# Hidden units in order in two expert stages, and routing choices made once behind the chunk loop

## The chip, the cores and the metric

The kernel runs on one core of a Trainium2 chip, as one program. The metric is the device time of one execution in microseconds, median of several runs. Everything is float32 unless a form says bf16.

## What is computed

Two layers, each a graph attention over 6250 nodes (256 features, 206250 edges) followed by a mixture of 8 experts, with residual additions. The change touches the expert halves only. Layer 0 takes the best two experts of a token, layer 1 the best one with a capacity per expert:

```python
logits = xt @ Wr + br                       # xt: 6250 x 256, Wr: 256 x 8
probs = softmax(logits); top_p, top_idx = top_k(probs, 2)
weights = top_p / top_p.sum(-1)
h = gelu((xn * ln_g + ln_b) @ W1[e] + b1[e])    # 256 -> 1024
y = h @ W2[e] + b2[e]                           # 1024 -> 256
out = sum of weights * y over the chosen experts
# layer 1: argmax of the softmax, relu in place of gelu, no scale and shift,
# tokens past the capacity of their expert are handled by position
```

## The kernel before, in words

The program is a sequence of phases: a plan of the edges, then per layer a node phase, an edge phase and `ffn_phases` (line 1272), which has two stages, routing and experts. Between stages all engines meet at a barrier.

**Routing** (lines 1292 to 1690). The 6250 tokens are 49 tiles of 128 (`NT`), in 7 chunks (`R`) of 7 tiles. SyncE loads the rows `xs` and the attention sums `ag` of a chunk (three `ag` buffers), stores the new rows (`keep_rows`, line 1358) and the scaled rows `xn` with their weights to `xb` (`keep_normed`, line 1362); its queue is one ordered list, so each store's wait holds the loads that stand behind it. GpSimd (POOL) adds the bias to each chunk (line 1420). VectorE runs `combine` (line 1519: sums divided, added to the rows, mean and variance) and `factors` (line 1547: scale and offset from ScalarE's root), and for the chunk before also `scores` (line 1560: logits, their maximum, the difference) and `choices` (line 1571: softmax, the chosen experts one-hot in `oh`, weights into `xn`, and `pick`). These work on 7 x 8 = 56 columns. In a chunk ScalarE takes the root (line 1469), the exponent of the chunk before (line 1473), scales 7 tiles (line 1482) and copies 7 transposed tiles out of PSUM (line 1488). Root and exponent need different tables, so each chunk has two table loads. TensorE transposes (line 1432) and makes the logits (line 1438).

Behind the loop TensorE counts the picks (lines 1451 and 1452), VectorE turns the counts into a slot for each choice (lines 1619 to 1648), and 7 chunks of one-hot matrices give the map from slots to tokens: `low` (line 1655), `low` times the token's lane as `lowp` (line 1657) and, per choice, `high` (line 1661), all on VectorE, two buffers each, multiplied on TensorE (lines 1460, 1461). Then come the block table and the map's decoding (lines 1663 to 1690).

**Experts** (lines 1692 to 1920). Tokens of one expert form blocks of 256 (`TB`). All engines loop over pairs of blocks, with two buffers of everything. SyncE loads a block's expert: `w1`, `w2`, `b1`, `b2` (lines 1742 to 1745), two blocks ahead, released by `s_yc` when VectorE has read a block's result. GpSimd gathers the tokens (line 1763), and scatters the result (line 1788 adds in DRAM in layer 0, line 1791 writes in layer 1). TensorE does per block 8 times 2 matmuls of the first product (line 1820), 4 transposes of the next block (line 1805) and 16 matmuls of the second (line 1831); the trace holds two records for each f32 matmul, so a block shows x32, x4 and x32. ScalarE applies the function with `b1` as bias (line 1843), VectorE scales the next block's transposes into `xT` (lines 1851, 1854), multiplies weights (`take`), adds `b2` (line 1896) and scales by the weight. In layer 1 it also replaces non-finite values (line 1914).

Hidden unit number p * 8 + j is unit p of group j. So each partition's part of `w2` and `b1` is one run in DRAM, and the stationary operand of line 1820 is every eighth column of `w1`:

```python
w1[:, k, c, :].rearrange("p (m j) -> p j m", j=FC)[:, j, :]       # line 1821
one(names["w2"]).rearrange("a (p j) d -> (a p) j d", j=FC)        # line 1743
one(names["b1"]).rearrange("a (p j) -> (a p) j", j=FC)            # line 1744
```

What sets the order: each engine's list is written out by hand, and semaphores are counted per block (`hold`, line 67). `done` (line 1495) makes VectorE wait for its own instruction.

Of the kernel before, what the change touches and what calls it, by code (L numbers as in the profile page):

```python
# [6 lines left out]
F32 = mybir.dt.float32  # L7
# [3 lines left out]
ALU = mybir.AluOpType  # L11
ACT = mybir.ActivationFunctionType
# [1259 lines left out]
def ffn_phases(nc, io, dr, layer, src, rows_in, out):  # L1272
# [13 lines left out]
    with ExitStack() as outer:  # L1286
# [5 lines left out]
        with ExitStack() as ctx:  # L1292
# [54 lines left out]
            s_w, s_const, s_zero, s_bias, s_agu, s_chain, s_stat, s_var, s_std, s_fac, s_xn = (  # L1347
                sem(n) for n in ("w", "const", "zero", "bias", "agu", "chain", "stat", "var", "std", "fac", "xn"))
            s_t, s_xT, s_l, s_soft, s_exp, s_wg, s_pick, s_cnt, s_low, s_lowp, s_map, s_done, s_kept = (
                sem(n) for n in ("t", "xT", "l", "soft", "exp", "wg", "pick", "cnt", "low", "lowp", "map", "done", "kept"))  # L1350
            block = ctx.enter_context(nc.Block())

            @block.sync
            def _(sp):
                tiles = lambda c: slice(c * R, (c + 1) * R)
                lines = lambda c: slice(c * R * P, (c + 1) * R * P)

                def keep_rows(c):
                    sp.wait_ge(s_agu, c + 1)
                    sp.dma_start(rows_in[lines(c), :].rearrange("(t p) d -> p t d", p=P), xs[:, tiles(c), :]).then_inc(s_kept, 16)  # L1360

                def keep_normed(c):
                    sp.wait_ge(s_wg, c + 1)
                    sp.wait_ge(s_xn, R * (c + 1))
                    sp.dma_start(xb[lines(c), :].rearrange("(t p) d -> p t d", p=P), xn[:, tiles(c), :]).then_inc(s_kept, 16)

                rest = N - (NT - 1) * P
                for c in range(R):
                    if first and c == R - 1:
                        sp.wait_ge(s_zero, 2)  # L1370
                        sp.dma_start(xs[:, c * R:NT - 1, :], src[c * R * P:(NT - 1) * P, :].rearrange("(t p) d -> p t d", p=P)).then_inc(s_x[c], 16)
                        sp.dma_start(xs[0:rest, NT - 1, :], src[(NT - 1) * P:N, :]).then_inc(s_x[c], 16)
                    else:
                        sp.dma_start(xs[:, tiles(c), :], src[lines(c), :].rearrange("(t p) d -> p t d", p=P)).then_inc(s_x[c], 16)
                    if c == 0:
                        sp.dma_start(bias[:, :], io["L0_gnn_bias" if first else "L1_gnn_bias"].partition_broadcast(P)).then_inc(s_w, 16)
                    if c >= AG:
                        keep_rows(c - AG)
                    sp.dma_start(ag[:, c % AG, :, :], dr["agg"][lines(c), :].rearrange("(t p) d -> p t d", p=P)).then_inc(s_ag[c % AG], 16)
                    if c == 0:  # L1380
                        sp.dma_start(wr[:, :, :], io[names["wr"]].rearrange("(c p) e -> p c e", p=P)).then_inc(s_w, 16)
                        sp.dma_start(br[:, :], io[names["br"]].partition_broadcast(P)).then_inc(s_w, 16)
                    if c > AG:
                        keep_normed(c - AG - 1)
                for c in range(R - AG, R):
                    keep_rows(c)
                    keep_normed(c - 1)
                sp.wait_ge(s_zero, 2)
                sp.dma_start(rows_in[NP:NP + TB, :].rearrange("(p s) d -> p (s d)", p=P), zero[:, :]).then_inc(s_kept, 16)
                keep_normed(R - 1)  # L1390
                sp.wait_ge(s_kept, 16 * (2 * R + 1))
# [31 lines left out]
            def _(pe):  # L1423
# [24 lines left out]

                pe.wait_ge(s_pick, R)
                picks = pick[:, :, :].rearrange("p t e -> p (t e)")  # L1450
# [14 lines left out]
            def _(act):  # L1465
# [4 lines left out]

                def powers(c):
                    act.wait_ge(s_soft, c + 1)
                    nc.scalar.activation(pr[:, c * R:(c + 1) * R, :], tmp[:, c * R:(c + 1) * R, :], ACT.Exp).then_inc(s_exp, 1)

                for c in range(R):
                    roots(c)
                    if c:
                        powers(c - 1)
                    act.wait_ge(s_fac, c + 1)
# [3 lines left out]
                    for k in range(R):  # L1483
# [4 lines left out]
                        nc.scalar.copy(xT[:, t % XP, :, :], ps_x[:, t % XP, 0:D].rearrange("p (c n) -> p c n", c=DC)).then_inc(s_xT, 1)  # L1488
                powers(R - 1)

            @block.vector
            def _(v):
# [63 lines left out]

                wide = lambda col: col.unsqueeze(2).to_broadcast([P, R, EXP])
                each = lambda row: row.unsqueeze(1).to_broadcast([P, R, EXP])

                def scores(c):  # L1560
                    cs = slice(c * R, (c + 1) * R)
                    v.wait_ge(s_l, R * (c + 1))
                    if first:
# [6 lines left out]

                def choices(c):
                    cs = slice(c * R, (c + 1) * R)
                    v.wait_ge(s_exp, c + 1)
                    p, q = pr[:, cs, :], tmp[:, cs, :]
# [33 lines left out]
                for c in range(R):  # L1608
                    combine(c)
                    if c:  # L1610
                        scores(c - 1)
                    factors(c)
                    if c:
                        choices(c - 1)
                scores(R - 1)
                choices(R - 1)
                v.wait_ge(s_cnt, 1)
# [32 lines left out]
                for c in range(R):  # L1650
                    k = c % 2
                    if c >= 2:
                        v.wait_ge(s_map, c - 1)
                    lows = slot[:, 2, c * R:(c + 1) * R, :].rearrange("p t n -> p (t n)")
                    done(nc.vector.tensor_tensor(low[:, k, :, :], iotal[:, :].unsqueeze(1).to_broadcast([P, R * top, P]),
                                                 lows.unsqueeze(2).to_broadcast([P, R * top, P]), ALU.is_equal))
                    nc.vector.tensor_scalar(lowp[:, k, :, :], low[:, k, :, :], iotan[:, 0:1], None, ALU.mult).then_inc(s_lowp, 1)
                    for j in range(R * top):
# [33 lines left out]
        with ExitStack() as ctx:  # L1692
# [5 lines left out]
            w1 = sb("w1", [P, 2, DC, FF], F32)  # L1698
            w2 = sb("w2", [P, 2, FC, D], F32)
            b1 = sb("b1", [P, 2, FC], F32)  # L1700
            b2 = sb("b2", [P, 2, D], F32)
# [21 lines left out]
            s_sc = [sem(f"sc{k}") for k in range(2)]  # L1723
            s_gx = [sem(f"gx{k}") for k in range(2)]
            s_gi, s_si, s_cur, s_add, s_mul, s_fl, s_pq, s_free = (sem(n) for n in ("gi", "si", "cur", "add", "mul", "fl", "pq", "free"))
            n_sc = 16 * SUB
            n_ldx = 16 * SUB
            n_ldw = 16 * 4
            n_ldg = 16 * 2
# [5 lines left out]
            def _(sp):  # L1735
                def load(b, k):
# [5 lines left out]
                    sp.dma_start(w1[:, k, :, :], one(names["w1"]).rearrange("a (p c) f -> (a p) c f", c=DC)).then_inc(s_ldw[k], 16)  # L1742
                    sp.dma_start(w2[:, k, :, :], one(names["w2"]).rearrange("a (p j) d -> (a p) j d", j=FC)).then_inc(s_ldw[k], 16)  # L1743
                    sp.dma_start(b1[:, k, :], one(names["b1"]).rearrange("a (p j) -> (a p) j", j=FC)).then_inc(s_ldw[k], 16)  # L1744
                    sp.dma_start(b2[:, k, :], one(names["b2"]).rearrange("a d -> (a d)").partition_broadcast(P)).then_inc(s_ldw[k], 16)

                for k in range(2):
                    load(k, k)
# [50 lines left out]
            def _(pe):  # L1799
                pe.wait_ge(s_const, 2)  # L1800

                def turn(k):
# [4 lines left out]
                    mm.then_inc(s_t, 1)  # L1807

                pe.wait_ge(s_ldx[0], n_ldx)
                turn(0)  # L1810
                pairs = pe.value_load(cnt_i[0:1, 0:1], min_val=1, max_val=(nblk_max + 1) // 2)
                with pe.Fori(0, pairs) as i:
                    for k in range(2):
                        hold(pe, s_ldw[k], i * n_ldw + n_ldw, s_pp)
                        hold(pe, s_xT, i * 2 + (k + 1), s_pp)
                        for j in range(FC):

                            hold(pe, s_act, i * (2 * FC) + (k * FC + j + 1), s_pp)
                            for c in range(DC):
                                mm = nc.tensor.matmul(ps_h[:, j % 4, 0:TB],  # L1820
                                                      w1[:, k, c, :].rearrange("p (m j) -> p j m", j=FC)[:, j, :],
                                                      xT[:, k, c, :], start=(c == 0), stop=(c == DC - 1))
# [24 lines left out]
            def _(v):  # L1847
# [9 lines left out]
                def take(b, k):  # L1857
# [5 lines left out]
                    nc.vector.tensor_tensor(wt[:, k, :], wt2[:, k, 0, :], wt2[:, k, 1, :], ALU.add)  # L1863

                def sources(b, k):
                    nc.vector.tensor_copy(gidx[:, k, :], who[:, bass.ds(b, 1), 0, :]).then_inc(s_gi, 1)
# [6 lines left out]
                for n, value in enumerate((0.0, 10000.0, -10000.0)):  # L1873
                    nc.vector.memset(bound[:, n, :], value).then_inc(s_fl, 1)
                v.wait_ge(s_fl, 3)
                v.sem_inc(s_yc, 1)
                v.wait_ge(s_t, 1)
                if first:
# [6 lines left out]
                with v.Fori(0, pairs) as i:  # L1885
                    for k in range(2):
                        hold(v, s_t, i * 2 + (k + 2), s_pv)
                        if first:
                            hold(v, s_ldg[1 - k], (i + k) * n_ldg + n_ldg, s_pv)
                        affine(1 - k)  # L1890
                        take(i * 2 + (k + 1), 1 - k)
# [74 lines left out]
```

## Time and profile before

| | |
|---|---|
| median of 3 runs | 6250.21 us (6245.75 to 6252.14) |
| the profiled execution | 6253.11 us |
| its span, first to last instruction | 6251.4 us |
| granted TensorE clock, mean | 0.883 |
| TensorE busy | 4504.6 us, 72% of the span |
| VectorE busy | 3544.0 us, 57% |
| ScalarE busy | 1454.2 us, 23% |
| GpSimd busy | 3674.1 us, 59% |

PE is TensorE's matmuls, PEld its weight loads, DVE VectorE, ACT ScalarE, POOL GpSimd, SP SyncE. The shares are means over stages with different limits: layer 0's routing lies from 2377 to 2584 us, its experts to about 3425, layer 1's routing from 5624 to 5795 and its experts to the end. Tile names in rows have the stage's prefix (`r_`, `x_`), out<-in. A timeline row merges neighbours of one line (xN).

### The profile page before, as it was taken

The numbers are of one execution on the slowest core, as the hardware profiler recorded it, in microseconds if no ns is written. First come the engines' busy times: TensorE is split into PE (matmuls) and PEld (weight loads), VectorE is DVE, ScalarE is ACT, GpSimd is POOL, SyncE is SP. The second block draws the span as 40 slices with busy tenths as digits, with TensorE's granted clock in tenths as the row PEclk, the third lists the DMA queues.
The fourth block names the chain that finished last, engine by engine and source line by source line (L and its number), as shares of the span: only waits on it lengthen the run. The fifth ranks groups of instructions, "written<-read, shape, count | busy, mean of one in ns | idle before, by whom it ended". The sixth has DMA issues, their size and how long they took to land. (4 is left out here: it accounts for less than half of the span.)

```text
span 6251.4 us, 96537 instructions
## 1 busy us (share of the span) xinstructions
PE 4504.6 (72%) x19217; PEld 3440.8 (55%) x19217; DVE 3544.0 (57%) x6578; ACT 1454.2 (23%) x3118; POOL 3674.1 (59%) x3755
## 2 busy tenths in 40 slices
PE   0678888888888885699998446565565655664898
PEld 0345555555555554599998334354453444554898
DVE  6678888888888877521221335344454443547444
ACT  1333333333333323122222201011110110113222
POOL 1577777777777751133333277777777777741333
PEclk9899999999999995799999668788787887885999
DMA  7566666666666644366666555555555555535555
GB/s 227 183 164 167 168 169 167 167 168 169 165 168 169 165 118 153 106 179 185 184 179 187 128 134 144 140 139 143 136 143 141 138 143 137 142 91 168 185 195 190
DMA packets 705207, 991.04 MB, mean 159 GB/s; under 512 B 300534, under 2 KB 520890, under 8 KB 682865
## 3 DMA queue, kind: packets, MB, share of 16 engines
q0 software_dynamic: 184848, 489.78, 31.0%
q1 hardware_dynamic: 513468, 484.16, 25.8%
q10 hardware_dynamic: 6564, 14.14, 0.7%
q14 instruction: 292, 2.38, 0.1%
q8 instruction: 35, 0.57, 0.0%
HBM read 868.78 MB, written 121.43 MB: 158 GB/s over the span
## 5 line engine op out<-in xcount | busy, mean ns | idle before, releaser
L782 POOL DMA_INDIRECT e_rows<-sc_table,e_eidx x3224 | 3082.0, 956 | 1013.6 <-issue 926.5
L888 PE MATMUL e_ps_o<-e_rows,e_oh 128*128 128x264 f32 x6344 | 1619.7, 400 | 46.9 <-DVE e_rows L1172 32.9
L888 PEld LDWEIGHTS e_ps_o<-e_rows,e_oh 128*128 128x128 f32 x6344 | 1218.9, 197 | 339.1 <-issue 115.0
L1172 DVE TENSOR_TENSOR e_rows<-e_rows,e_ps_w 128x1024 f32<-128x1024 f32 x806 | 969.2, 1206 | 5.3 <-ACT e_rows L984 5.2
L991 ACT COPY e_res<-e_ps_o 32x264 f32<-32x264 f32 x793 | 291.0, 367 | 1864.7 <-PE e_ps_o L894 1454.3
L858 PE MATMUL e_ps_X<-e_ident,e_alog 128*104 128x128 f32 x496 | 96.1, 356 | 773.2 <-ACT e_alog L968 773.2
L1820 PE MATMUL x_ps_h<-x_xT,x_w 128*128 128x256 f32 x2624 | 647.0, 405 | 5.2 <-DMA x_b<-in_L_ffn_b_dram 5.2
L1820 PEld LDWEIGHTS x_ps_h<-x_xT,x_w 128*128 128x128 f32 x2624 | 637.9, 337 | 9.6 <-issue 5.9
L1831 PE MATMUL x_ps_y<-x_w,x_hT 128*128 128x256 f32 x2624 | 580.0, 380 | 0.0
L964 ACT ACTIVATE e_encr<-e_ps_enc 128x512 f32<-128x512 f32 x806 | 473.5, 591 | 397.8 <-PE e_ps_enc L817 383.1
L1831 PEld LDWEIGHTS x_ps_y<-x_w,x_hT 128*128 128x128 f32 x2624 | 494.5, 191 | 62.0
L858 PEld LDWEIGHTS e_ps_X<-e_ident,e_alog 128*104 128x104 f32 x496 | 81.0, 230 | 799.9 <-issue 799.9
L1091 DVE TENSOR_SCALAR e_ohT<-e_at,e_nid 96x512 bf16<-96x512 int16 x806 | 293.9, 365 | 321.8 <-DMA e_aw<-sc_a2p 205.5
L1843 ACT ACTIVATE x_hT<-x_ps_h,x_b 128x256 f32<-128x256 f32 x656 | 304.8, 473 | 736.5 <-PE x_ps_h L1820 736.2
L1125 DVE TENSOR_TENSOR e_ps_k<-e_ps_X,e_y 104x512 f32<-104x512 f32 x31 | 21.7, 700 | 795.0 <-ACT e_y L972 795.0
L829 PE MATMUL e_ps_X<-e_u,e_hwide 128*104 128x512 f32 x806 | 415.5, 596 | 54.2 <-DVE e_u L1105 54.2
L817 PE MATMUL e_ps_enc<-e_at,e_w_enc 96*128 96x512 bf16 x806 | 312.1, 387 | 188.3 <-DVE e_u L1099 110.2
L894 PE MATMUL e_ps_o<-e_res,e_sel 128*128 128x264 f32 x1464 | 447.8, 388 | 0.0
L1763 POOL DMA_INDIRECT x_xin<-sc_xb,x_gidx x176 | 173.6, 987 | 448.0 <-issue 414.2
L1099 DVE SCALAR_TENSOR_TENSOR e_u<-e_encr,e_adst,e_ps_hd 128x512 f32<-128x512 f32 x403 | 297.3, 738 | 84.6 <-ACT e_encr L964 79.4
L1105 DVE TENSOR_TENSOR e_u<-e_u,e_ps_hd 128x512 f32<-128x512 f32 x403 | 277.4, 688 | 111.5 <-DVE e_ps_hd L1101 106.2
L1101 DVE SCALAR_TENSOR_TENSOR e_ps_hd<-e_encr,e_adst,e_ps_hd 128x512 f32<-128x512 f32 x403 | 301.3, 748 | 41.2 <-ACT e_encr L964 38.1
(332 smaller groups left out, 4677.1 us busy)
## 6 DMA issues: line engine op xcount, KB each, us to landing
x_w<-in_L_ffn_W_dram SPq DMA_DIRECT2D x112, 1024.0 KB
e_at<-sc_grp SPq DMA_DIRECT2D x403, 192.0 KB
x_w<-in_L_ffn_w_dram SPq DMA_DIRECT2D x60, 1024.0 KB
e_rows<-sc_table,e_eidx POOLq DMA_INDIRECT x3224
e_at<-sc_grp SPq DMA_DIRECT2D x403, 96.0 KB
sc_agg<-e_res SPq DMA_DIRECT2D x816, 33.0 KB
e_fr<-sc_rec SPq DMA_DIRECT2D x62, 312.2 KB
e_hp<-sc_hp SPq DMA_DIRECT2D x403, 48.0 KB
```

Of the source, the lines that this page charges most:

```text
L782: pool.indirect_dma_start(rows[:, k, s, j, :], None, dr["table"][:, :], bass.IndirectOffsetOnAxis(eidx[:, k, s, j:j + 1], 0)).then_inc(s_r ...
L817: nc.tensor.matmul(ps_enc[:, h, :], half(w_enc[:, :], h), at[:, ring(s), 0, :].bitcast(BF16), start=True, stop=True).then_inc(s_enc, 1)
L829: nc.tensor.matmul(ps_X[0:COLS, :], hwide[:, COLS - HEADS * (s + 1):2 * COLS - HEADS * (s + 1)], u[:, par(s), :], start=(s == 0), stop=Fal ...
L888: nc.tensor.matmul(place, oh[:, k, at_j:at_j + P], rows[:, k, s, j, :], start=(j == 0), stop=False)
L894: nc.tensor.matmul(place, sel[:, k, s * WIN:s * WIN + P], seen, start=False, stop=True).then_inc(s_o, 1)
L964: nc.scalar.activation(encr[:, h, :], ps_enc[:, h, :], ACT.Relu).then_inc(s_relu, 1)
L1099: nc.vector.scalar_tensor_tensor(u0[:, p, :], encr[:, 0, :], adst[:, 0:1], ps_hd[:, 0, :], ALU.add, ALU.mult).then_inc(s_u, 1)
L1101: nc.vector.scalar_tensor_tensor(ps_hd[:, 1, :], encr[:, 1, :], adst[:, 1:2], ps_hd[:, 1, :], ALU.add, ALU.mult).then_inc(s_u1, 1)
L1172: nc.vector.tensor_tensor(part, part, ps_w[:, k, :, s * HEADS:(s + 1) * HEADS].unsqueeze(3).to_broadcast([P, CH, HEADS, DH]), ALU.mult).th ...
L1820: mm = nc.tensor.matmul(ps_h[:, j % 4, 0:TB], w1[:, k, c, :].rearrange("p (m j) -> p j m", j=FC)[:, j, :], xT[:, k, c, :], start=(c == 0), ...
L1831: mm = nc.tensor.matmul(ps_y[:, s, 0:D], hT[:, k, j, s * P:(s + 1) * P], w2[:, k, j, :], start=(j == 0), stop=(j == FC - 1))
L1843: nc.scalar.activation(hT[:, k, j, :], ps_h[:, j % 4, 0:TB], ACT.Gelu if first else ACT.Relu, bias=b1[:, k, j:j + 1]).then_inc(s_act, 1)
```

## The change

Experts: hidden unit number j * 128 + m is now unit m of group j, so line 1821 reads 128 neighbouring columns, and `w2` arrives as eight runs of 1 KB per partition. The load of `b1` per block goes. Instead all experts' `b1` are loaded once as 64 rows of 128, transposed by TensorE, copied by VectorE to `b1c`, and `hidden_bias` picks 8 columns of it per block on VectorE, with a register load for the expert's number, ahead of the scaled transposes.

Routing: `scores`, the exponent and `choices` run once for all 49 tiles, behind the chunk loop. The stores of `xn` all move behind the choices. The multiplication for `lowp` moves from VectorE to ScalarE, and VectorE no longer waits for `low`.

```diff
                 def keep_normed(c):
-                    sp.wait_ge(s_wg, c + 1)
                     sp.wait_ge(s_xn, R * (c + 1))
...
-                    if c > AG:
-                        keep_normed(c - AG - 1)
                 for c in range(R - AG, R):
                     keep_rows(c)
-                    keep_normed(c - 1)
...
-                keep_normed(R - 1)
+                sp.wait_ge(s_wg, 1)
+                for c in range(R):
+                    keep_normed(c)
...
-                pe.wait_ge(s_pick, R)
+                pe.wait_ge(s_pick, 1)
...
                 for c in range(R):
                     roots(c)
-                    if c:
-                        powers(c - 1)
...
-                powers(R - 1)
+                act.wait_ge(s_soft, 1)
+                nc.scalar.activation(pr[:, :, :], tmp[:, :, :], ACT.Exp).then_inc(s_exp, 1)
+                for c in range(R):
+                    k = c % 2
+                    act.wait_ge(s_lowv, c + 1)
+                    if c >= 2:
+                        act.wait_ge(s_map, c - 1)
+                    nc.scalar.activation(lowp[:, k, :, :], low[:, k, :, :], ACT.Copy, scale=iotan[:, 0:1]).then_inc(s_lowp, 1)
...
-                def scores(c):
-                    cs = slice(c * R, (c + 1) * R)
-                    v.wait_ge(s_l, R * (c + 1))
+                def scores():
+                    cs = slice(0, NT)
+                    v.wait_ge(s_l, NT)
...
                     combine(c)
-                    if c:
-                        scores(c - 1)
                     factors(c)
-                    if c:
-                        choices(c - 1)
-                scores(R - 1)
-                choices(R - 1)
+                scores()
+                choices()
...
-                    done(nc.vector.tensor_tensor(low[:, k, :, :], iotal[:, :].unsqueeze(1).to_broadcast([P, R * top, P]),
-                                                 lows.unsqueeze(2).to_broadcast([P, R * top, P]), ALU.is_equal))
-                    nc.vector.tensor_scalar(lowp[:, k, :, :], low[:, k, :, :], iotan[:, 0:1], None, ALU.mult).then_inc(s_lowp, 1)
+                    nc.vector.tensor_tensor(low[:, k, :, :], iotal[:, :].unsqueeze(1).to_broadcast([P, R * top, P]),
+                                            lows.unsqueeze(2).to_broadcast([P, R * top, P]), ALU.is_equal).then_inc(s_lowv, 1)
...
-                    sp.dma_start(w2[:, k, :, :], one(names["w2"]).rearrange("a (p j) d -> (a p) j d", j=FC)).then_inc(s_ldw[k], 16)
-                    sp.dma_start(b1[:, k, :], one(names["b1"]).rearrange("a (p j) -> (a p) j", j=FC)).then_inc(s_ldw[k], 16)
+                    sp.dma_start(w2[:, k, :, :], one(names["w2"]).rearrange("a (j p) d -> (a p) j d", j=FC)).then_inc(s_ldw[k], 16)
...
+                sp.dma_start(b1r[:, :], io[names["b1"]].rearrange("e (j m) -> (e j) m", m=P)).then_inc(s_b1, 16)
                 for k in range(2):
                     load(k, k)
...
+                pe.wait_ge(s_b1, 16)
+                nc.tensor.transpose(ps_y[:, 0, 0:EXP * FC], b1r[:, :], ident[0:EXP * FC, 0:EXP * FC]).then_inc(s_b1t, 1)
                 pe.wait_ge(s_ldx[0], n_ldx)
                 turn(0)
...
-                                                      w1[:, k, c, :].rearrange("p (m j) -> p j m", j=FC)[:, j, :],
+                                                      w1[:, k, c, j * P:(j + 1) * P],
...
+                def hidden_bias(b, k):
+                    e = v.value_load(tab_i[0:1, bass.ds(b, 1)], min_val=0, max_val=EXP - 1)
+                    nc.vector.tensor_copy(b1[:, k, :], b1c[:, bass.ds(e * FC, FC)])
...
+                v.wait_ge(s_b1t, 1)
+                nc.vector.tensor_copy(b1c[:, :], ps_y[:, 0, 0:EXP * FC]).then_inc(s_b1t, 1)
+                v.wait_ge(s_b1t, 2)
                 v.sem_inc(s_yc, 1)
+                hidden_bias(0, 0)
...
                         hold(v, s_t, i * 2 + (k + 2), s_pv)
                         if first:
                             hold(v, s_ldg[1 - k], (i + k) * n_ldg + n_ldg, s_pv)
+                        hidden_bias(i * 2 + (k + 1), 1 - k)
                         affine(1 - k)
```

## Rows read from the trace of the kernel before

**Rows 1.** Windows: us, PE, PEld, DVE, ACT, POOL busy, granted clock, DMA share, GB/s

```profile
2610.00:3400.00 790.00, 790.00 (x3571) 746.77 (x3570) 157.63 (x580) 225.09 (x443) 272.78 (x210) 1.00 0.61 182
5716.00:5741.00 25.00, 18.20 (x84) 16.40 (x84) 20.91 (x63) 17.88 (x38) 0.00 (x0) 0.50 0.45 148
```

**Rows 2.** Chain that ended last, layer 1's experts: start us, us, engine and line

```profile
5807.31 9.70 PE x_ps_h L1820 x32
5824.38 7.67 PE x_ps_h L1820 x32
5832.52 6.91 PE x_ps_y L1831 x32
5839.43 7.68 PE x_ps_h L1820 x32
```

**Rows 3.** Page's costliest groups: count, busy us, mean ns, idle us before

```profile
L1820 PE MATMUL x_ps_h<-x_xT,x_w 128*128 128x256 f32 x2624 | 647.0, 405 | 5.2 <-DMA x_b<-in_L_ffn_b_dram 5.2
L1820 PEld LDWEIGHTS x_ps_h<-x_xT,x_w 128*128 128x128 f32 x2624 | 637.9, 337 | 9.6 <-issue 5.9
L1831 PEld LDWEIGHTS x_ps_y<-x_w,x_hT 128*128 128x128 f32 x2624 | 494.5, 191 | 62.0
```

**Rows 4.** Groups of weight loads, layer 1's experts, the transposes' row

```profile
L1805 PEld LDWEIGHTS x_ps_x<-x_ident,x_xin 128*128 128x128 f32 x108 | 17.2, 203 | 1.0
```

**Rows 5.** TensorE timeline, layer 0's experts: start us, us, line, operation

```profile
3006.60 7.84 PE L1820 MATMUL x_ps_h<-x_xT,x_w 128*128 128x256 f32 x32
```

**Rows 6.** DMA, 3000 to 3030 us, 40 slices: busy tenths of 16 engines

```profile
DMA  9999300023410195999999996000234101949999
```

**Rows 7.** Hardware queue, 2500 to 2580 us: packets, MB, share of 16 engines

```profile
q1 hardware_dynamic: 2893, 3.04, 11.0%
```

**Rows 8.** POOL's waits, layer 0 experts: us in total, times, longest

```profile
POOL sc_x L1788 <- DVE x_y L1901: 108.8, 51, 4.3
```

**Rows 9.** Register load on SyncE: ns min/median/max, first and last start us

```profile
L1737 SPq TENSOR_LOAD <-f_tab_i x86: 269/278/459, 2584.3 to 6231.9; - x86
```

**Rows 10.** VectorE timeline, layer 0's chunk loop: start us, us, line, operation

```profile
2410.73 0.17 DVE L1555 SCALAR_TENSOR_TENSOR r_off<-r_mean,r_fac 128x7 f32<-128x7 f32 x1
2457.77 3.63 DVE L1555 SCALAR_TENSOR_TENSOR r_off<-r_mean,r_fac 128x7 f32<-128x7 f32 x1
2465.99 0.18 DVE L1510 TENSOR_SCALAR r_ag<-r_ag 128x56 f32<-128x56 f32 x1
2474.56 0.17 DVE L1507 TENSOR_TENSOR r_var<-r_var,r_tmp 128x7 f32<-128x7 f32 x1
2507.07 0.17 DVE L1555 SCALAR_TENSOR_TENSOR r_off<-r_mean,r_fac 128x7 f32<-128x7 f32 x1
```

**Rows 11.** Timeline, ScalarE, layer 0's chunk loop

```profile
2409.95 0.31 ACT L1469 ACTIVATE r_std<-r_var,r_eps 128x14 f32<-128x14 f32 x1 [31.50 <-DVEq L1545]
2476.59 3.54 ACT L1482 ACTIVATE r_xn<-r_xs,r_off,r_fac 128x256 f32<-128x256 f32 x7
2485.54 0.37 ACT L1488 COPY r_xT<-r_ps_x 128x256 f32<-128x256 f32 x1 [0.80 <-PE r_ps_x L1432]
```

**Rows 12.** Timeline, VectorE, layer 1's chunk loop, first and last factors

```profile
5657.02 0.17 DVE L1555 SCALAR_TENSOR_TENSOR r_off<-r_mean,r_fac 128x7 f32<-128x7 f32 x1
5737.66 0.17 DVE L1555 SCALAR_TENSOR_TENSOR r_off<-r_mean,r_fac 128x7 f32<-128x7 f32 x1
```

**Rows 13.** Timelines of VectorE and TensorE behind the chunk loops

```profile
2518.77 0.22 DVE L1507 TENSOR_TENSOR r_lg<-r_ps_l,r_std 128x56 f32<-128x56 f32 x1 [6.39 <-PE r_ps_l L1438]
2524.88 1.02 PE L1451 MATMUL r_ps_c<-r_pick,r_upper 128*128 128x392 f32 x1 [6.15 <-DVE r_pick L1593]
5760.02 0.57 DVE L1507 TENSOR_TENSOR r_tmp<-r_pos,r_oh 128x392 f32<-128x392 f32 x1
```

**Rows 14.** VectorE timeline, layer 0's map: a scaled low row, the next low row

```profile
2545.17 0.69 DVE L1657 TENSOR_SCALAR r_lowp<-r_low,r_iotan 128x1792 bf16<-128x1792 bf16 x1
2548.45 2.02 DVE L1655 TENSOR_TENSOR r_low<-r_iotal,r_slot 128x1792 bf16<-128x1792 f32 x1
```

More of the change, by code:

```diff
@@ L1348, in ffn_phases @@
                 sem(n) for n in ("w", "const", "zero", "bias", "agu", "chain", "stat", "var", "std", "fac", "xn"))
+            s_lowv = sem("lowv")
             s_t, s_xT, s_l, s_soft, s_exp, s_wg, s_pick, s_cnt, s_low, s_lowp, s_map, s_done, s_kept = (
@@ L1469, in roots @@
                     nc.scalar.activation(std[:, 0:n, c * R:(c + 1) * R], var[:, 0:n, c * R:(c + 1) * R], ACT.Sqrt, bias=eps[:, 0:1]).then_inc(s_std, 1)
-                def powers(c):
-                    act.wait_ge(s_soft, c + 1)
-                    nc.scalar.activation(pr[:, c * R:(c + 1) * R, :], tmp[:, c * R:(c + 1) * R, :], ACT.Exp).then_inc(s_exp, 1)
                 for c in range(R):
                     roots(c)
-                    if c:
-                        powers(c - 1)
                     act.wait_ge(s_fac, c + 1)
@@ L1555, in factors @@
                     nc.vector.scalar_tensor_tensor(off[:, cs], mean[:, cs], -1.0, fac[:, cs], ALU.mult, ALU.mult).then_inc(s_fac, 1)
-                wide = lambda col: col.unsqueeze(2).to_broadcast([P, R, EXP])
-                each = lambda row: row.unsqueeze(1).to_broadcast([P, R, EXP])
-                def scores(c):
-                    cs = slice(c * R, (c + 1) * R)
-                    v.wait_ge(s_l, R * (c + 1))
+                wide = lambda col: col.unsqueeze(2).to_broadcast([P, NT, EXP])
+                each = lambda row: row.unsqueeze(1).to_broadcast([P, NT, EXP])
+                def scores():
+                    cs = slice(0, NT)
+                    v.wait_ge(s_l, NT)
                     if first:
@@ L1569, in scores, with choices @@
                     nc.vector.tensor_tensor(tmp[:, cs, :], lg[:, cs, :], wide(c1[:, 0, cs]), ALU.subtract).then_inc(s_soft, 1)
-                def choices(c):
-                    cs = slice(c * R, (c + 1) * R)
-                    v.wait_ge(s_exp, c + 1)
+                def choices():
+                    cs = slice(0, NT)
+                    v.wait_ge(s_exp, 1)
                     p, q = pr[:, cs, :], tmp[:, cs, :]
@@ L1699, in ffn_phases @@
             w2 = sb("w2", [P, 2, FC, D], F32)
+            b1r = sb("b1r", [EXP * FC, P], F32)
+            b1c = sb("b1c", [P, EXP * FC], F32)
             b1 = sb("b1", [P, 2, FC], F32)
@@ L1724, in ffn_phases @@
             s_gx = [sem(f"gx{k}") for k in range(2)]
+            s_b1, s_b1t = sem("b1"), sem("b1t")
             s_gi, s_si, s_cur, s_add, s_mul, s_fl, s_pq, s_free = (sem(n) for n in ("gi", "si", "cur", "add", "mul", "fl", "pq", "free"))
@@ L1727, in ffn_phases @@
             n_ldx = 16 * SUB
-            n_ldw = 16 * 4
+            n_ldw = 16 * 3
             n_ldg = 16 * 2
```

## The prediction

> **What bounds the kernel now.** Read the stages first: in layer 0's experts TensorE is busy for all of 790.00 us at a granted clock of 1.00, while in layer 1's chunk loop it is busy for 18.20 of 25.00 us at 0.50 [rows 1]. So the experts are bound by TensorE and the routing by something else. The chain that ended last shows an expert block: 7.67 us of line 1820, 0.47 of transposes, 6.91 of line 1831, one block per 15.05 us (5824.38 to 5839.43) with no wait in between [rows 2]. Both products are 16 matmuls of one size, so a matmul costs 480 ns in the first and 432 in the second. The costliest groups show where they differ: the weight load, 337 ns against 191, at the same shape [rows 3]. TensorE waited for 5.2 us in all of line 1820 [rows 3]. Line 1820 picks its weights with a step of eight words, line 1831 without one; the transposes, which pick theirs with a step of two, load in 203 ns [rows 4]. The step of eight is the suspect for the 48 ns.
>
> **Experts: line 1820 in order.** After the edit both products have the same operand shapes and steps. I take 6.91 us for the first as well, so a block is 6.91 + 0.47 + 6.91 = 14.29 us, 0.76 less. There are 2624/32 = 82 blocks [rows 3]; the first of each layer runs at a lower clock (9.70 us [rows 2]) and I leave them out: 80 x 0.76 = **-61**. Bounds: 0, if the 48 ns are not the load's, and no more than this, since line 1831 is the fastest f32 product of this size here.
>
> [...]
>
> What the shorter block leans on. **Weights:** the second weights' DMA goes from one 8 KB run per partition to eight runs of 1 KB, 1024 pieces. Rows of about 1 KB cost 0.110 x 80 us x 16 / 2893 = 49 ns of one engine [rows 7], so 1024 on 16 engines take 3.1 us. The load released by the end of one block lies in the busy stretch from 3009.75 to 3018.75 (0.75 us a slice), 9 us for 2.1 MB [rows 6], so this tensor has about 4 us now. The change is between -1 and +3.1; I take +0.5, less what the 128 pieces of 32 bytes of the dropped bias load took. The block that needs it starts at 3006.60 [rows 5] + 15.05 = 3021.65, 2.9 us after the load's end; 0.76 and 0.5 of that go, 1.6 stay, so TensorE still doesn't wait. **POOL:** in layer 0 it waits 108.8/51 = 2.13 us per block for VectorE's scaled rows [rows 8]; no row tells how much of it is its own start after the release, so I put the spare at 1 to 2 us, and 0.76 go. **Bias pick:** the nearest row to VectorE's register load is SyncE's, 278 ns [rows 9]; with index arithmetic and one copy of eight columns I take 1 us per block, bounds 0.4 and 2. It stands ahead of the scaled transposes, which need 1 us and have the whole second product, 6.91 us [rows 2], until TensorE needs them. That cover hides it; without it, it would cost 82 us. Behind it on VectorE stand the take and the next gather's indices, for which POOL waits; those rows are gathered three blocks ahead, so 1 us there has blocks of cover. The start of each stage gets one more small load and loses one, waits for the same large weights, and has one transpose under them: +0.5 each, **+1**, bounds 0 and 3.
>
> **Routing, chunk loop.** In layer 0 from the first factors to the last it takes 2507.07 - 2410.73 = 96.3 us for six chunks [rows 10], in layer 1 80.6 [rows 12]. A VectorE chunk without choices is 2465.99 to 2474.73, 8.74 us [rows 10], and 0.95 more from ScalarE's root at 2409.95 to the offsets' end at 2410.90 [rows 10, 11]: 9.7. Without scores and exponents ScalarE loses both table loads of a chunk and does: seven scalings and seven copies, 2476.59 to 2485.91, 9.32 us [rows 11]; then from the root to the next scaling 0.95 and two hand-overs, some 0.07: 10.34. ScalarE (paced by TensorE's transposes) becomes the bound by 0.6 us. Three of the six chunks also meet a POOL bias add, which holds VectorE: a 0.17 us operation took 3.63 [rows 10]. I take 9 us for the three together, bounds 0 and 12. Layer 0: 3 x 10.34 + 3 x 9.7 + 9 = 69.1, gain **-27** (24 to 34). Layer 1 has three short operations fewer, about 0.6: ScalarE 10.1, VectorE 9.1: 30.4 + 27.3 + 9 = 66.7, gain **-14** (10 to 19). The row loads still arrive in time: they are issued earlier, since SyncE no longer stands at the choices.
>
> **Routing, choices behind the loop.** The last chunk's scores and choices now take 2518.77 to 2524.88, 6.1 us for 24 operations of 56 columns or fewer and one exponent, 0.25 each [rows 13]. At 392 columns an operation takes 0.57 [rows 13], 0.60 with the gap to the next. Layer 0: 19 wide x 0.60 + 5 short x 0.23 + 0.6 for the exponent = 13.1, **+7**. Layer 1: 11 x 0.60 + 2 x 0.23 + 0.6 = 7.7 against 13 x 0.25 = 3.3, **+4**. The exponent's table load goes ahead of its wait, under the last logits. The seven stores of scaled rows move behind the choices: 6.3 MB, at 49 ns per row on 16 engines 6272 x 49 / 16 = 19 us, under the counting and the map: in layer 1 there are still 47 us from 5760.02 [rows 13] to the first block at 5807.31 [rows 2]. SyncE issues nothing else there. Bounds 0 and, if the stage ended before they land, +5.
>
> **Routing, low rows.** VectorE loses 0.69 us [rows 14] seven times, in layer 1, at half the columns, I take 0.45; less 0.09 of overlap each, plus a wait per chunk: **-7**. On ScalarE a scaled copy of 256 columns takes 0.51 (3.54/7 [rows 11]); 1792 columns are at most seven of those, 3.5 us, under VectorE's remaining 4.7 per chunk (5.3 now: 2.02 for the low rows and 2545.17 to 2548.45 [rows 14]). TensorE's maps start later, but only the last chunk's tail counts, and the block table (some 3 us) covers it. Bounds 0 and -8.
>
> **Sum.** -61 + 1 - 27 - 14 + 7 + 4 - 7 = -97. The profiled execution took 6253.1; minus 97 is 6156. It lies 2.9 above the median of the runs, so I predict **6153 us**.
>
> **Rivals.** (a) The load is hidden anyway: line 1820 stays at 480 ns for another reason, such as its moving operand. For: 337 ns would fit under 480. Against: line 1831 at equal sizes. Gain 36: 6214. (b) Layer 0's experts gain only part: the scatter ahead of POOL's gather or the weights become the bound once 0.76 us of a 1.3 us reserve are gone. At 14.7 us per block, 54 x 0.4 = 22 are lost: 6175. (c) Denser work lifts the clock in the chunk loop: 0.73 busy (18.20 of 25 us [rows 1]) times 80.6/66.7 is 0.88, between the stretch at 0.50 and the one at 1.00 with its full 790. The copies then wait less, but VectorE is close behind: 3 x 0.6 and 3 x 1.0 in the chunks and about as much behind the last, some 10 us: 6143. (d) The combined loop is bound by transfers and gains nothing: 41 us lost, 6194; against it, the DMA share there was 0.45 [rows 1]. (e) **Slower:** the 1 KB pieces of the second weights are late and TensorE waits in every block. It decides from 16.1 us per block in layer 0, where 54 x 1.05 uses up the other gains (21 of layer 1's experts and 36 of routing). The load now ends 12.1 us after the block end that releases it (3006.60 [rows 5] to 3018.75 [rows 6]), so the second weights would have to take 4 us more than now, 8 in place of 3.1: 125 ns per piece against 49 [rows 7]. At 16.4 us per block: 6266.
>
> **Chances.** Forecast 0.68 (its own range 6140 to 6168, from the bounds of the chunk loop and the low rows), (a) 0.09, (b) 0.10, (c) 0.08, (d) 0.02, (e) 0.03. The range runs from 6135 to 6185: it takes in (b) and (c) and leaves out (a), (d), (e), 0.14. A difference under 0.2% (12.5 us) can't be told from none. Faster 0.96, within 0.2% 0.01 (between (e) and the rest), slower 0.03.
>
> **What would show it.** Right: line 1820's load near 191 ns, its share of a block 6.9 us, blocks 14.3 apart in both layers; one table load between roots and exponent; offsets 10.3 apart in late chunks of layer 0; 392-column choices of about 13 and 8 us; maps about 4.7 us apart. Wrong: loads shorter but blocks still 15 apart, TensorE idle in the experts waiting for weights, POOL no longer waiting for line 1901, or a block end held by the late stores.

## The result, and the profile after the change

The changed kernel takes **6148.49 us** (median of 6 runs, 6142.27 to 6152.39), the kernel before 6249.71 (6 runs): a ratio of 0.9838, 95% interval 0.9825 to 0.985, so 101 us less where 97 were forecast. The profiled execution of the changed kernel took 6152.39 us, with a span of 6150.6.

Lines have moved a little: the first product is line 1821 and the second 1832. The page's costliest groups first (count, busy us, mean ns, idle us before):

```profile
L1821 PE MATMUL x_ps_h<-x_xT,x_w 128*128 128x256 f32 x2624 | 584.0, 381 | 7.4 <-DMA x_b<-in_L_ffn_b_dram 7.0
...
L1821 PEld LDWEIGHTS x_ps_h<-x_xT,x_w 128*128 128x128 f32 x2624 | 501.0, 191 | 77.7 <-issue 8.9
L1832 PEld LDWEIGHTS x_ps_y<-x_w,x_hT 128*128 128x128 f32 x2624 | 492.9, 190 | 63.5
```

Against [rows 3]: the load fell from 337 ns to the other product's value, and in 82 blocks TensorE waited only 7.4 us ahead of this line, 7.0 of them for a transfer at the starts of the two stages. The chain of layer 1's experts (start us, us, what) gives the block:

```profile
5741.59 6.91 PE x_ps_h L1821 x32
...
5748.96 6.91 PE x_ps_y L1832 x32
5755.87 6.91 PE x_ps_h L1821 x32
...
6000.43 6.71 DMA x_xr<-sc_x,x_sidx
...
6015.10 6.89 DMA x_xr<-sc_x,x_sidx
```

Blocks are 14.28 us apart (5741.59 to 5755.87) in place of 15.05 [rows 2]. From about 6000 us the chain runs over another loop: gathered rows, their final addition, the store, the next gather, 14.67 us around in these rows. That is already longer than TensorE's 14.28, so a still shorter product should gain little in layer 1; no run tries it.

The windows (us, PE, PEld, DVE, ACT, POOL busy, granted clock, DMA share, GB/s), of layer 0's experts and layer 1's routing, answer to [rows 1]:

```profile
2610.00:3360.00 750.00, 734.97 (x3498) 649.50 (x3496) 161.81 (x624) 220.30 (x433) 271.00 (x208) 0.99 0.68 193
5560.00:5720.00 160.00, 72.83 (x397) 65.45 (x397) 120.14 (x273) 51.72 (x114) 33.95 (x13) 0.50 0.57 175
```

In the first window TensorE has done its last block at 3345.2 us, and up to there it is busy almost without a break (0.2 us idle from 2610). The clock in layer 1's routing stays at 0.50 (second row). The timelines of VectorE, ScalarE and TensorE there (start us, us, line, operation):

```profile
2411.29 0.17 DVE L1556 SCALAR_TENSOR_TENSOR r_off<-r_mean,r_fac 128x7 f32<-128x7 f32 x1
...
2467.50 0.17 DVE L1556 SCALAR_TENSOR_TENSOR r_off<-r_mean,r_fac 128x7 f32<-128x7 f32 x1
2477.72 0.17 DVE L1556 SCALAR_TENSOR_TENSOR r_off<-r_mean,r_fac 128x7 f32<-128x7 f32 x1
...
5590.31 0.17 DVE L1556 SCALAR_TENSOR_TENSOR r_off<-r_mean,r_fac 128x7 f32<-128x7 f32 x1
...
5654.07 0.17 DVE L1556 SCALAR_TENSOR_TENSOR r_off<-r_mean,r_fac 128x7 f32<-128x7 f32 x1
...
2487.26 1.28 ACT L1484 ACT_TABLE_LOAD   x1
2491.63 0.53 ACT L1484 ACTIVATE r_pr<-r_tmp 128x392 f32<-128x392 f32 x1 [3.09 <-DVE r_tmp L1570]
...
2489.23 0.57 DVE L1508 TENSOR_TENSOR r_lg<-r_ps_l,r_std 128x392 f32<-128x392 f32 x1 [11.35 <-PE r_ps_l L1437]
...
2502.96 1.67 PE L1450 MATMUL r_ps_c<-r_pick,r_upper 128*128 128x392 f32 x2 [13.77 <-DVE r_pick L1594]
...
5665.59 0.57 DVE L1508 TENSOR_TENSOR r_lg<-r_ps_l,r_br 128x392 f32<-128x392 f32 x1 [11.35 <-PE r_ps_l L1437]
...
5673.35 1.67 PE L1450 MATMUL r_ps_c<-r_pick,r_upper 128*128 128x392 f32 x2 [7.80 <-DVE r_pick L1597]
...
2515.85 2.02 DVE L1652 TENSOR_TENSOR r_low<-r_iotal,r_slot 128x1792 bf16<-128x1792 f32 x1
2520.47 2.02 DVE L1652 TENSOR_TENSOR r_low<-r_iotal,r_slot 128x1792 bf16<-128x1792 f32 x1
```

First to last offsets: 66.4 us in layer 0 and 63.8 in layer 1, 96.3 and 80.6 before [rows 10, 12]. There is one table load behind the loop, under the last logits. The choices at 392 columns take 13.7 us (2489.23 to 2502.96) and 7.8. The map's chunks are 4.62 us apart.

With the stages cut at POOL's first memset of routing, the first expert matmul and the start of the last block, the profiled executions differ as follows (us):

| | before | after | difference |
|---|---|---|---|
| layer 0 routing | 220.9 | 193.1 | -27.8 |
| layer 0 experts | 799.8 | 760.0 | -39.8 |
| graph stages between | 2226.1 | 2226.8 | +0.7 |
| layer 1 routing | 183.3 | 167.7 | -15.6 |
| layer 1 experts, to the last block | 408.2 | 387.5 | -20.7 |
| last block to the end | 35.9 | 37.9 | +2.0 |

What the prediction counted on hiding behind other work stayed hidden. The bias pick, in VectorE's timeline of layer 1's experts, is 0.87 us of idle time for the register and 0.18 of copy:

```profile
6082.40 0.18 DVE L1868 COPY x_b<-x_b1c 128x8 f32 x1 [0.87 <-issue]
```

The stores of the scaled rows, from 2501.67 us, fill the DMA engines until about 2526 (first below the issue, then the busy tenths of 16 engines from 2500 to 2560 in 40 slices); the first expert matmul is at 2570.75. They take 24 us, where 19 were forecast, and are done well before it:

```profile
2501.67 14.12 SPq L1365 DMA_DIRECT2D sc_xb<-r_xn  x7
...
DMA  0299999999999999400000000000000000000000
```

### The profile page after: what moved, and what is told of

The parts are those of the page before. It is cut to its first block and busy times, and to the rows that moved or that the text cites. A ratio compares the mean times of both kernels' runs of the same rounds, so it can differ in the third digit from the quotient of the medians.

```text
span 6150.6 us, 96530 instructions
## 1 busy us (share of the span) xinstructions
PE 4441.1 (72%) x19219; PEld 3313.0 (54%) x19219; DVE 3507.4 (57%) x6429; ACT 1447.0 (24%) x3100; POOL 3689.8 (60%) x3755
## 5 line engine op out<-in xcount | busy, mean ns | idle before, releaser
L1821 PE MATMUL x_ps_h<-x_xT,x_w 128*128 128x256 f32 x2624 | 584.0, 381 | 7.4 <-DMA x_b<-in_L_ffn_b_dram 7.0
L1821 PEld LDWEIGHTS x_ps_h<-x_xT,x_w 128*128 128x128 f32 x2624 | 501.0, 191 | 77.7 <-issue 8.9
```

Of the source, the lines that this page charges most:

```text
L1821: mm = nc.tensor.matmul(ps_h[:, j % 4, 0:TB], w1[:, k, c, j * P:(j + 1) * P], xT[:, k, c, :], start=(c == 0), stop=(c == DC - 1))
```

## The experiments

**The two halves, each alone.** The kernel before with the experts' edits, and with routing's.

> The kernel before with the experts' half of the change alone (first weights picked in order, second weights as eight runs of 1 KB, biases picked on VectorE); routing as before. Theory: the step of eight in the first product's weights cost 48 ns per matmul, and nothing in routing takes part. Blocks 14.28 us apart in place of 15.05 in both layers, chunk loops 96 and 81 us as before, so the experts' part of the gain alone: 39.8 + 20.7 less some 2 at the end, about -59, near 6191 us. Rival A (the routing half also feeds the experts, by earlier weights or an earlier stage start): blocks between 14.4 and 15.0, gain under 45. Rival B (the halves share a gain, such as the clock's): gain well over 70.

> The kernel before with the routing half alone (choices once behind the loop, scaled low rows on ScalarE); experts as before. Theory: the gain of routing is its own: layer 0's chunk loop 66 us in place of 96, layer 1's 64 in place of 81, the choices behind the loop 14 and 8 us, routing stages shorter by 28 and 16: about -43, near 6207 us, blocks 15.05 apart. The two halves then sum to the whole of -101. Rival (the halves depend on each other): they miss the sum by over 10 us.

Measured: the experts' half 6189.84 us (ratio 0.9903, 0.9887 to 0.992), 59.6 less than 6249.48; routing's half 6202.54 (0.9925, 0.9908 to 0.9942), 46.9 less. Blocks are 14.28 us apart in the first kernel and 15.05 in the second; layer 0's routing takes 220.9 us in the first and 192.8 in the second. The halves sum to 106.6 against 101.2 for the whole, which lies within their intervals, and in each kernel the untouched half keeps the values of the kernel before: no dependence shows between them.

**The step of the stationary operand.** Three kernels change only how line 1821 picks its 128 units: with a step of 8, 4 or 2. The edit for 8 is shown; the other two are slices with that step.

```
-  w1[:, k, c, j * P:(j + 1) * P],
+  w1[:, k, c, :].rearrange("p (m j) -> p j m", j=FC)[:, j, :],
```

> The changed kernel with one edit: the first weights are picked with a step of eight again, as before; the second weights' 1 KB runs and the bias pick stay. So a hidden unit meets another unit's bias and second weights. Theory (the step is what costs): loads of 337 ns, first product 7.67 us per block, blocks 15.05 apart, 80 x 0.77 = 62 us slower than the changed kernel, near 6210. Rival (the gain came with the form of the second weights or of the bias, or with the moving operand): 191 ns, blocks 14.28, 6148.

> The changed kernel with the first weights picked with a step of four words (16 bytes) in groups of 512 units; a hidden unit meets another unit's bias and second weights. The transposes with a step of two loaded in 203 ns and step eight in 337, step one in 191. Theory 1 (a price per step, linear beyond two): about 203 + (337 - 203)/3 = 248 ns, and the matmul pitch of 216 ns per record (432 per matmul) grows only by some 8 to 32, blocks 14.4 to 14.8, time 6160 to 6190. [...] Theory 3 (only steps beyond four cost): about 200 ns, blocks 14.28, 6148.

> The changed kernel with the first weights picked with a step of two words in groups of 256 units; a hidden unit meets another unit's bias and second weights. Step one loaded in 191 ns, step four in 330, step eight in 337. [...]

The groups of the page, for step 8, step 4 and step 2:

```profile
L1821 PEld LDWEIGHTS x_ps_h<-x_xT,x_w 128*128 128x128 f32 x2624 | 637.8, 337 | 11.2 <-issue 7.4
```

```profile
L1821 PEld LDWEIGHTS x_ps_h<-x_xT,x_w 128*128 128x128 f32 x2688 | 638.5, 330 | 11.0 <-issue 7.5
```

```profile
L1821 PEld LDWEIGHTS x_ps_h<-x_xT,x_w 128*128 128x128 f32 x2624 | 517.8, 198 | 61.9 <-issue 7.9
```

So loads take 191, 198, 330 and 337 ns at steps 1, 2, 4 and 8. The one line with step 8 brings back 15.05 us per block, with the 1 KB runs and the bias pick in place: the step was the whole of the experts' loss. Its time was 6202.02 us rather than 6210: against the profiled execution of the changed kernel its blocks cost 60.6 us more, but layer 0's routing began 6.9 us sooner, behind stages that the edit doesn't touch, and the end from the last block on was 2.4 shorter. Step 4 gives blocks of 14.87 us and 6225.72; the other values that it computes fill two more blocks in layer 1 (2688/32 = 84), and without 2 x 14.87 it is 6196: theory 1 (248 ns, blocks of 14.8 at most) and theory 3 (200 ns) both fall. Step 2 gave 6149.71, level with the changed kernel. The first product takes 6.91 us per block at steps 1 and 2, 7.50 at step 4 and 7.67 at step 8: 216, 234 and 240 ns per record. The 132 ns of load between steps 2 and 4 cost 18 ns per record, the 7 between steps 4 and 8 cost 5. So up to 198 ns a load cost nothing here, and from 330 to 337 it cost for the most part; where in between that begins, and why the load jumps between steps 2 and 4, no run shows.

**Transfers: room for the second weights and for short pieces.** One kernel loads the second weights in 8 KB runs again; the other loads each block's biases by a transfer and drops the pick on VectorE (the count of awaited transfers, not shown, grows by that one).

```
-  one(names["w2"]).rearrange("a (j p) d -> (a p) j d", j=FC)
+  one(names["w2"]).rearrange("a (p j) d -> (a p) j d", j=FC)
```

```
+  sp.dma_start(b1[:, k, :], one(names["b1"]).rearrange("a (j p) -> (a p) j", p=P)).then_inc(s_ldw[k], 16)
-  hidden_bias(0, 0)
-  hidden_bias(i * 2 + (k + 1), 1 - k)
```

> The changed kernel with the second weights loaded in one 8 KB run per partition, as before; hidden units meet other units' second weights. Theory (the 1 KB runs cost little and lie beside the matmuls): blocks stay 14.28 us apart and the time at 6148, and the block's transfers fall off at most 1 us earlier or 3 us earlier by the two bounds of the prediction, by 0.5 as it took it. Rival (the second weights are on the path): blocks under 14.2.

> The changed kernel with the hidden biases loaded per block by a transfer of 1024 words to their partitions in place of the pick on VectorE (the one load, transpose and copy ahead of the loop stay). It asks how much room the weights' transfers have: in the changed kernel a block's load is issued from 2989.6 us and its transfers fall off near 3000.0, 1.8 us ahead of the matmul at 3001.83. Theory (a short piece costs what the 1 KB rows cost, 49 ns on one engine): 1024 / 16 x 49 ns = 3.1 us more, 1.3 more than the room, so blocks of 15.6 us in both layers and 80 x 1.3 = 104 us slower than the changed kernel, near 6252: the pick on VectorE is then what lets the units stand in order. Rival A (a word's piece costs under 28 ns): hidden, 6148. Rival B (125 ns and over, as in my slower case): 8 us more, blocks over 20 us, over 6600.

One block's load, 12.66 us from its first issue in 40 slices of 0.317 us: busy tenths of the DMA engines, then the hardware queue (packets, MB, share of 16 engines). The changed kernel, the one with 8 KB runs, and the one with biases by transfer:

```profile
DMA  1740119283999989979999999999999940000000
...
q1 hardware_dynamic: 1616, 2.23, 54.6%
```

```profile
DMA  0952119747899999989999999899997300000000
```

```profile
DMA  5001019777789999968999999999999999200000
...
q1 hardware_dynamic: 2656, 2.23, 60.7%
```

The last busy slice is the 33rd, the 32nd with 8 KB runs and the 35th with the words: about 10.3, 9.9 and 10.8 us behind the issue. So the 1 KB runs cost some 0.4 us, little more than a slice, and with 1.8 us of room they cost no time: blocks are 14.28 us apart with the 8 KB runs too, and 6172.26 us less two more blocks in layer 1, which the other values fill, is 6143.7. The words' theory fell. 1040 more packets took (0.607 - 0.546) x 12.66 x 16 = 12.4 us of engines, 12 ns each and not 49. They stay hidden but for a little: 6146.03 us, layer 1's blocks at 14.28, but layer 0's between 14.27 and 14.96 and its experts' stage 2.2 us longer (762.2 against 760.0). So the units could stand in order without the pick on VectorE, and the pick costs nothing that shows.

**Scaled low rows back on VectorE.** VectorE also waits for `low` again, and ScalarE's loop goes (not shown).

```
-  nc.scalar.activation(lowp[:, k, :, :], low[:, k, :, :], ACT.Copy, scale=iotan[:, 0:1]).then_inc(s_lowp, 1)
+  nc.vector.tensor_scalar(lowp[:, k, :, :], low[:, k, :, :], iotan[:, 0:1], None, ALU.mult).then_inc(s_lowp, 1)
```

> The changed kernel with the scaled low rows back on VectorE. Theory (VectorE paces the map, and the move freed it): chunks of the map 5.34 us apart in layer 0 in place of 4.62 and 3.08 in layer 1 in place of 2.59, so 7 x 0.72 + 7 x 0.49 = 8.5 us slower than the changed kernel, near 6157; the rest of the stage as it was. Rival (TensorE or the transfers behind it set the end of the stage): pitch as said but the first expert matmul no later, 6148.

VectorE's timeline in the map of layer 0, then of layer 1:

```profile
2511.73 2.02 DVE L1645 TENSOR_TENSOR r_low<-r_iotal,r_slot 128x1792 bf16<-128x1792 f32 x1
2513.79 0.69 DVE L1647 TENSOR_SCALAR r_lowp<-r_low,r_iotan 128x1792 bf16<-128x1792 bf16 x1
2517.08 2.02 DVE L1645 TENSOR_TENSOR r_low<-r_iotal,r_slot 128x1792 bf16<-128x1792 f32 x1
...
5686.13 1.09 DVE L1645 TENSOR_TENSOR r_low<-r_iotal,r_slot 128x896 bf16<-128x896 f32 x1
...
5689.22 1.08 DVE L1645 TENSOR_TENSOR r_low<-r_iotal,r_slot 128x896 bf16<-128x896 f32 x1
```

Chunks are 5.35 and 3.09 us apart, the stages 6.3 and 3.4 us longer, the time 6155.51. So VectorE paces the map with the multiplication on it, the stages' ends move with it (the rival falls), and the move was worth 9.7 us by the stages, 8.5 by the pitches and 7.0 by the times.

**What the chunk loop lost: tables or choices?** An exponent of one column per chunk brings back the table loads alone.

```
 roots(c)
+if c:
+    nc.scalar.activation(junk[:, 0:1], eps[:, 0:1], ACT.Exp)
```

> The changed kernel with one exponent of a single column added to ScalarE behind the root of every chunk but the first; nothing reads it, and it waits for nothing. It brings back the two table loads per chunk without the scores and choices, and so parts the chunk loops' gain in two. Theory (ScalarE paces the changed loop, so the loads are paid in full): 2 x 1.28 + 0.2 = 2.8 us more per chunk, 13.0 us in layer 0 and 12.8 in layer 1 where no add of POOL is met; loops of 78 to 83 us in layer 0 and 77 to 81 in layer 1, in place of 66.4 and 63.8: 26 to 34 us slower than the changed kernel, 6175 to 6182. Then the tables are nearly all of layer 1's gain (its loop took 80.6 before) and about half of layer 0's (96.3), whose other half is the choices on VectorE. Rival (the loads fall into ScalarE's waits, and what the loop lost was VectorE's choices): loops under 70 and 67, under 6156.

ScalarE's timeline in layer 0's loop:

```profile
2466.38 1.28 ACT L1469 ACT_TABLE_LOAD   x1
2467.67 0.31 ACT L1469 ACTIVATE r_std<-r_var,r_eps 128x14 f32<-128x14 f32 x1
2468.00 1.28 ACT L1475 ACT_TABLE_LOAD   x1
2469.29 0.20 ACT L1475 ACTIVATE r_junk<-r_eps 128x1 f32<-128x1 f32 x1
2469.40 3.54 ACT L1479 ACTIVATE r_xn<-r_xs,r_off,r_fac 128x256 f32<-128x256 f32 x7
...
2478.74 1.28 ACT L1469 ACT_TABLE_LOAD   x1
```

Chunks are 12.36 us apart in both layers, the loops 73.6 and 73.5 us, the time 6168.11: neither theory's number. 2.15 and 2.36 us per chunk are paid of 2.8, since part of the second load lies where ScalarE waited for VectorE's factors (in layer 0 it starts at 2468.00, and the offsets end at 2468.62); and POOL's adds no longer lengthen a chunk (73.6 us for six are 12.3 each). So the tables, added to the changed loop, cost 7.2 us of the 29.9 by which layer 0's loop fell and 9.7 of layer 1's 16.8. What is left, 22.7 and 7.1 us, went with the scores, choices and waits for the exponent; that part is had by difference and wasn't run alone. It also holds the chunks that POOL's adds had stretched. The kernel before shows this (VectorE's offsets, and one of POOL's adds); below it stand offsets of the kernel with the one-column exponent:

```profile
2491.63 0.17 DVE L1555 SCALAR_TENSOR_TENSOR r_off<-r_mean,r_fac 128x7 f32<-128x7 f32 x1
...
5685.11 0.17 DVE L1555 SCALAR_TENSOR_TENSOR r_off<-r_mean,r_fac 128x7 f32<-128x7 f32 x1
5700.47 0.17 DVE L1555 SCALAR_TENSOR_TENSOR r_off<-r_mean,r_fac 128x7 f32<-128x7 f32 x1
5712.85 0.17 DVE L1555 SCALAR_TENSOR_TENSOR r_off<-r_mean,r_fac 128x7 f32<-128x7 f32 x1
...
5696.30 3.96 POOL L1420 TENSOR_TENSOR r_xs<-r_xs,r_bias 128x1792 f32<-128x1792 f32 x1 [11.41 <-DMA r_xs<-sc_x]
```

```profile
5630.85 0.17 DVE L1559 SCALAR_TENSOR_TENSOR r_off<-r_mean,r_fac 128x7 f32<-128x7 f32 x1
5643.20 0.17 DVE L1559 SCALAR_TENSOR_TENSOR r_off<-r_mean,r_fac 128x7 f32<-128x7 f32 x1
```

In layer 1 a chunk without an add took 12.38 us before and takes 12.35 with the tables alone: there the tables are the whole difference to 10.0, and most of the 7.1 us lies in two chunks that met an add (15.36 us for the one shown). In layer 0 a chunk without an add took 15.44 before (2491.63 to 2507.07 [rows 10]), 12.36 with the tables and 10.2 without, so scores and choices cost it 3.1 us and the tables 2.15.

**A version that is faster than both.** In the changed kernel the first chunk's operations stand beside POOL's bias adds (VectorE's timeline):

```profile
2387.30 3.87 DVE L1511 TENSOR_SCALAR r_valid<-r_iotan 128x49 f32<-128x49 f32 x1 [8.65 <-DMA r_br<-in_L_ffn_br_dram]
2391.20 3.88 DVE L1511 TENSOR_SCALAR r_ag<-r_ag 128x56 f32<-128x56 f32 x1
...
2395.66 5.17 DVE L1508 TENSOR_TENSOR r_ag<-r_ag 128x1792 f32<-128x1792 f32 x1
```

The edit gives the adds to VectorE, for all seven chunks (shown) or for the first three (c < 3). POOL's loop starts behind them, and VectorE waits for POOL's adds only from there (neither shown):

```
+  if c < 7:
+      v.wait_ge(s_x[c], 32 if first and c == R - 1 else 16)
+      tt(rows, rows, bias[:, :].unsqueeze(1).to_broadcast([P, R, D]), ALU.add)
```

> The changed kernel with one edit that aims past it: the bias of the graph stage is added to all chunks' rows on VectorE, and POOL adds none. In the changed kernel the first chunk's four operations on VectorE, from 2387.30 to 2406.53, take 3.87, 3.88, 5.17 and 5.67 us beside POOL's adds, where the same ones take 0.17, 0.18, 2.02 and 2.02 in later chunks, and later adds of POOL hold it for 2.2, 1.3 and 3.2 us. Theory (POOL's adds hold VectorE): the first chunk ends 14.2 - 2.1 = 12 us earlier in each layer; the chunks behind it are VectorE's, 9.7 + 2.06 = 11.8 us apart in layer 0 and 11.2 in layer 1, so the loops take 70.6 and 67 us in place of 66.4 and 63.8: each routing stage 8 us shorter, 16 in all, near 6132. Rival A (the first chunk waits for its loads anyway): its end stays, and the loops' growth is all that shows, 7 us slower, 6156. Rival B (the long operations are long for another reason, such as loads that write the same memory): 3.9 to 5.7 us again, and about 20 us slower.

> The same edit for the first three chunks alone; POOL adds the bias to the other four. Theory: the first chunk 12 us earlier; two chunks at 11.8, one of them held some 3 us by POOL's add for the fourth chunk, which starts as soon as its rows have landed; the last four as in the changed kernel. Loops of about 69 and 66 us, each stage 8 to 10 us shorter: 6129 to 6133, level with the variant that adds all on VectorE, since an add on VectorE costs 2.06 us and one on POOL holds VectorE for 1.3 to 3.2. Rival (POOL's fourth add now falls beside the first chunk and holds it as long as three did): gain under 5 us in each stage, over 6138.

With all seven, the same operations read:

```profile
2382.98 0.19 DVE L1511 TENSOR_SCALAR r_valid<-r_iotan 128x49 f32<-128x49 f32 x1 [8.71 <-DMA r_br<-in_L_ffn_br_dram]
2383.21 0.19 DVE L1511 TENSOR_SCALAR r_ag<-r_ag 128x56 f32<-128x56 f32 x1
...
2383.97 2.02 DVE L1508 TENSOR_TENSOR r_ag<-r_ag 128x1792 f32<-128x1792 f32 x1
2386.03 2.02 DVE L1508 TENSOR_TENSOR r_xs<-r_xs,r_bias 128x1792 f32<-128x1792 f32 x1
```

Its time is **6127.87 us**, ratio 0.9809 (0.9795 to 0.9822) to the kernel before: some 20 us under the changed kernel, whose interval (0.9825 to 0.985) it doesn't meet. The stages are 7.9 and 10.1 us shorter, so 18 us are the edit's. The first chunk ends 12.0 and 11.8 us sooner, as the theory had it, and its operations are short: rivals A and B fall. Chunks are 11.75 and 10.9 apart. With three chunks, 6138.04 (0.9827, 0.9814 to 0.984, which overlaps the changed kernel's interval): a POOL add beside the second chunk holds one operation for 5.82 us, that loop takes 75.8 us in layer 0, where 69 were expected, and the stages are 1.9 and 6.9 us shorter in place of 8 to 10. The theory had one hold of 3 us in that chunk; two came (5.82 and, some us later, 5.67 in place of 2.02 each), 7.4 us together. Adds on VectorE at 2.02 us are cheaper than POOL's, which held it for 3.8 and 3.65 us in that chunk.

## Why the prediction was right

**Experts, -61: right.** The two layers' blocks give -39.8 and -20.7. The cause was the load, as the step-8 run shows, so rival (a) falls: loads of the same 128 columns take 191 ns in order and 337 with a step of eight. They are hidden beside matmuls in part: 146 ns more of load cost 24 ns per record (240 against 216), all of it past step 2's 198 ns.

**What the block leans on: right.** The 1 KB runs took 0.4 us for the 0.5 taken, and 1.8 us of room was left for the 1.6 forecast. The bias pick takes about 1 us, as taken, and TensorE shows no wait for it (0.2 us idle in 735 of layer 0's experts). The +1 for the stages' starts didn't show: with the experts' half alone, the stretches up to the first expert matmul took 220.9 and 182.5 us, 220.9 and 183.3 before. Rival (b) falls with blocks of 14.28 in layer 0, (e) with it. The 49 ns per piece that priced (e) were measured on rows of about 1 KB [rows 7]; words cost 12.

**Chunk loops, -27 and -14: right in mechanism, 2.7 and 2.9 too small.** The mis-sized term is the three chunks with POOL adds, taken at VectorE's 9.7 and 9.1 us and 9 us of hold together. Undisturbed chunks take 10.2 and 10.0, as forecast for ScalarE's bound (10.34 and 10.1); six of these leave only 5.1 and 3.8 us for the adds. The three chunks that met an add took 35.8 and 33.8 us together, where 38.1 and 36.3 were forecast. Rival (c) falls with the clock at 0.50, (d) with the shorter loops.

**Choices, +7 and +4: right** (13.7 and 7.8 us for 13.1 and 7.7). **Low rows, -7: right in kind**, 8.5 by the pitches. The end was not in the sum: +2.0 from the last block on, where the chain runs over layer 1's slower loop of gathers and stores. In all -101 for -97, the difference mostly the loops' 5.6; the smaller misses partly cancel, which is luck.

## What to carry to other kernels

Read the weight load's mean by line before blaming the matmul: two groups of one shape and different means (337 and 191 ns here) can point to the access step, and an experiment on the step alone settles it. Take loops that alternate two ScalarE functions apart (here two table loads of 1.28 us per chunk), but price the saving from what each engine would wait for next, not from the loads' sum (2.15 and 2.36 us were paid of 2.8). And look for short operations that take as long as another engine's long one (3.87 us for 49 columns beside POOL's adds of 3.93): there the work may be cheaper on the engine that is held (2.02 us an add).

## What had not been expected

The load's time jumps between steps 2 and 4 (198 to 330 ns) and hardly grows behind (337 at 8). A transferred word cost 12 ns of a DMA engine, where rows of 1 KB cost 49 [rows 7]. An operation of 49 columns took 3.87 us beside POOL's adds, about one whole add (11.78 us for three), and 0.19 without them, while one of 1792 columns took 5.17 and 2.02: 3.7 and 3.2 us more, whatever the length. That fits a hold for about a whole add and not a slowing in proportion.
